# Value tiles in two alternating buffers, and a new order of jobs in the loop of a fused attention and mixture-of-experts kernel

## The reference

```python
xn = _layernorm(x, axis=-1)
x = x + _L0_attn_ref(xn, ...) + _L0_ffn_ref(xn, ...)

# _L0_attn_ref: 16 heads of 16, causal
score = softmax(Q @ K.T / sqrt(16) + mask);  out = (score @ V) @ WO

# _L0_ffn_ref: 16 heads of 64, 8 experts, top 2 of them
q, k = _rope(xn @ Wq), _rope(xn @ Wk)
gv = _gate(x, Wsel_v)                       # sigmoid, top-2 mask, (b, h, s, e)
v = jnp.einsum('bsd,bhse,hedp->bhsp', x, gv, Wv)
att = jax.nn.softmax(q @ k.T / np.sqrt(P), axis=-1)
o = jnp.einsum('bhst,bhtp->bhsp', att, v)
go = _gate(x, Wsel_o)
src2 = jnp.einsum('bhsp,bhse,hepd->bsd', o, go, Wo)
src = _ln(src + src2, ln1_g, ln1_b)
return _ln(src + relu(src @ W1 + b1) @ W2 + b2, ln2_g, ln2_b)
```

## Time and profile before

| | us |
|---|---|
| median of 3 runs (lowest, highest) | 3324.17 (3323.59, 3324.88) |
| the profiled execution, its own time | 3322.09 |
| span of its trace | 3320.0 |
| busy: PE, PE weight load | 3194.8 (96%), 2394.5 (72%) |
| busy: DVE, ACT, POOL | 2459.3 (74%), 2006.3 (60%), 1578.1 (48%) |

### The profile page before, as it was taken

One profiled execution on the slowest core, in us unless ns is written; L12 is line 12 of the kernel. 1 busy time (PEld: TensorE's weight loads), 2 busy tenths in 40 slices (PEclk: granted clock), 3 DMA queues, 4 the chain that ended last, 5 costly groups with the idle time before them and its releaser, 6 DMA issues.

```text
span 3320.0 us, 67575 instructions
## 1 busy us (share of the span) xinstructions
PE 3194.8 (96%) x19648; PEld 2394.5 (72%) x19648; DVE 2459.3 (74%) x4686; ACT 2006.3 (60%) x4635; POOL 1578.1 (48%) x1295
## 2 busy tenths in 40 slices
PE   4899999999999999999999999999999999998997
PEld 3677777777777777777777777777777777776887
DVE  7677777777777777777777777777777777776896
ACT  4566665666666666666666666666666666565443
POOL 5243554335543554435543454435544444435777
PEclk8999999999999999999999999999999999999999
DMA  5232332333233332333333332333323333333222
GB/s 191 72 89 70 104 94 75 85 92 99 70 86 77 100 98 67 89 88 99 81 75 85 93 99 70 86 95 95 86 67 89 88 99 82 74 83 107 85 84 77
DMA packets 116199, 294.21 MB, mean 89 GB/s; under 512 B 33856, under 2 KB 54592, under 8 KB 99776
## 3 DMA queue, kind: packets, MB, share of 16 engines
q1 hardware_dynamic: 116160, 293.73, 33.8%
...
## 4 chain that ended last, share of the span: by engine, by line
PE 71%; DVE 19%; issue 6%; ACT 1%; POOL 1%; DVEq 0%; DMA 0%; SPq 0%; POOLq 0%; ACTq 0%
PE bank L760 24%; PE bank L903 14%; PE bank L818 9%; PE bank L876 7%; PE bank L775 5%; DVE nmax L1350 4%; PE bank L847 2%; DVE vm L1371 2%; PE bank L780 2%; PE bank L888 2%; DVE vm L1414 2%; DVE uf L1458 2%; PE bank L1011 2%; PE bank L856 2%; DVE vm L1396 1%
## 5 line engine op out<-in xcount | busy, mean ns | idle before, releaser
L616 POOL TENSOR_TENSOR u_l<-uf,u_h 128x512 fp32r<-128x512 f32 x508 | 683.5, 1356 | 716.0 <-ACT u_h L1183 716.0
L1350 DVE TENSOR_REDUCE nmax<-bank 128x1 f32<-128x512 f32 (+3 forms) x1024 | 552.5, 580 | 374.2 <-PE bank L775 368.5
L760 PE MATMUL bank<-wv_h,xx 128*128 128x512 f32 x2048 | 745.6, 410 | 11.2 <-DVE vm L1371 5.9
L1093 ACT ACTIVATE probs<-bank,nmax 128x512 f32<-128x512 f32 (+3 forms) x1024 | 590.7, 610 | 258.5 <-DVE nmax L1350 258.5
L1183 ACT ACTIVATE u_h<-uf 128x512 fp32r<-128x512 f32 x508 | 320.5, 631 | 652.5 <-DVE uf L1458 504.5
L760 PEld LDWEIGHTS bank<-wv_h,xx 128*128 128x128 f32 x2048 | 386.7, 189 | 192.0 <-issue 69.3
L611 POOL TENSOR_TENSOR v_sb<-v_next,zero_hb 128x512 f32<-128x512 f32 x64 | 74.6, 1166 | 876.0 <-PE bank L876 876.0
L903 PE MATMUL bank<-u_h,wo_h 128*128 128x512 f32 x1016 | 429.8, 423 | 32.7 <-issue 27.2
L818 PE MATMUL bank<-ident_sb,probs 128*128 128x128 f32 x3328 | 451.1, 274 | 2.3 <-ACT pt_e L1113 1.2
L818 PEld LDWEIGHTS bank<-ident_sb,probs 128*128 128x128 f32 x3328 | 386.6, 141 | 69.1 <-issue 13.3
L1458 DVE TENSOR_TENSOR uf<-oo,go 128x512 f32<-128x512 f32 x508 | 420.3, 837 | 2.6 <-POOL u_l L616 0.4
...
## 6 DMA issues: line engine op xcount, KB each, us to landing
go<-go_d SPq DMA_DIRECT2D x256, 512.0 KB, 6.5
...
oo<-scale_d SPq DMA_DIRECT2D x128, 128.0 KB, 2.9
a_d<-a_out SPq DMA_DIRECT2D x128, 128.0 KB, 2.3
...
go_d<-go_turned SPq DMA_DIRECT2D x256, 8.0 KB
```

The lines of the kernel that those rows point to most:

```text
L616: nc.gpsimd.tensor_tensor(low, full, high.bitcast(f32), ALU.subtract).then_inc(ul_done, 1)
L760: last = nc.tensor.matmul(out, lhs, rhs, start=n == 1, stop=n == 3 * len(chunks))
L1093: nc.scalar.activation(probs[:, s % 2, j, 0:w], sbank[j][:, 0:w], ACT.Exp, bias=nmax[:, 2 * s + j:2 * s + j + 1], **kw).then_inc(exp_done, 1)
L1350: nc.vector.tensor_reduce(nmax[:, 2 * s + j:2 * s + j + 1], sbank[j][:, 0:w], AX.X, ALU.max, negate=True).then_inc(nmax_ready, 1)
```

## The change

Two things are changed.

**The value tiles.** `v_next` is gone and `v_sb` gets a leading index of two. VectorE adds up the values of the next pass straight into `v_sb[:, odd]`, and `AT` reads the other half. The copy `VC` on GpSimd and its semaphore are gone; `AT` waits for VectorE's sums themselves (`v_ready`). As the index is a constant in the code, the loops of TensorE and VectorE step by two and hold two bodies each, 31 times round instead of 62. ScalarE's, GpSimd's and SyncE's loops stay as they are.

**The tables.** The jobs are the same but for `VC`; their places are new. On TensorE by step:

| step | before | after |
|---|---|---|
| 0 | P0 P1 P2 P3 AT AC | P0 P1 P2 P3 AT |
| 1 | V0 V1 | AC V0 V1 J0 |
| 2 | J0 J1 | J1 |
| 3 | V2 J2 V3 | V2 J2 J3 |
| 4 | J3 J4 V4 | V3 |
| 5 | QK0 J5 QK1 | V4 QK0 J4 QK1 |
| 6 | V5 J6 V6 | J5 V5 V6 |
| 7 | V7 ST0 ST1 J7 | V7 ST0 J6 ST1 J7 |

VectorE has U2 in step 1 behind CH1 (before: step 2), V0 and U3 in step 2, U4 V1 U5 in step 3, V2 V3 in step 4, V4 U6 QL0 U7 QL1 in step 5, V5 V6 in step 6, V7 in step 7. ScalarE has PA between `a_out` (AC) and UH1 in step 0, nothing in steps 1 and 3, UH2 UH3 in step 2, UH4 UH5 in step 4, QH0 PB UH6 QH1 VA VN in step 5, UH7 in step 6. GpSimd has no part in the steps' softmax, so only its order counts: UL0 UL1 RP0 UL2 UL3 RP1 RS UL4 UL5 RA UL6 PC UL7 (before: VC UL0 UL1 UL2 RP0 UL3 RP1 UL4 RS RA UL5 UL6 PC UL7).

The diff, with the tables cut to a line or two:

```diff
--- before.py
+++ after.py
@@ -37,37 +37,37 @@
 BEHIND = ("AT", "AC", "ON", "U", "UH", "UL", "J", "YA")
 AHEAD = ("P", "V", "QK", "ST", "QH", "QL", "SO", "RP", "RS", "PA", "PB", "RA", "PC", "VN", "SQ", "SK", "EX", "CH")
 
-PE_FILL = [[("P", 0), ("P", 1), ("P", 2), ("P", 3), ("AT", 0), ("AC", 0)],
...
+PE_FILL = [[("P", 0), ("P", 1), ("P", 2), ("P", 3), ("AT", 0)],
+           [("AC", 0), ("V", 0), ("V", 1), ("J", 0)],
...
 V_ORDER = [(0, 0), (0, 1), (1, 0), (1, 1), (0, 2), (0, 3), (1, 2), (1, 3)]
 
@@ -185,8 +185,7 @@
         k_h = sb("k_h", [NP, S], f32r)
         k_l = sb("k_l", [NP, S], f32r)
         vm = sb("vm", [NP, 2, S])
-        v_next = sb("v_next", [NP, TT, 2, P])
-        v_sb = sb("v_sb", [NP, TT, 2, P])
+        v_sb = sb("v_sb", [NP, 2, TT, 2, P])
         va_next = sb("va_next", [NP, TT, 2, CA])
         va = sb("va", [NP, TT, 2, STRIP])
         nmax = sb("nmax", [NP, UNITS])
@@ -304,7 +303,6 @@
         stack_ready = sem("stack_ready")
         pool_step = sem("pool_step")
         v_ready = sem("v_ready")
-        vc_ready = sem("vc_ready")
         va_ready = sem("va_ready")
         part_high = sem("part_high")
         va_next_ready = sem("va_next_ready")
@@ -604,12 +602,7 @@
 
                 def do(job):
                     name, e = job
-                    if name == "VC":
-                        if kind != FIRST:
-                            pool.wait_ge(w_full, w_at(kind, it, ("AT", 0))[2] + 1)
-                        pool.wait_ge(v_ready, it * 8 + 8)
-                        nc.gpsimd.tensor_tensor(v_sb[:].rearrange("q t j c -> q (t j c)"), v_next[:].rearrange("q t j c -> q (t j c)"), zero_hb[:], ALU.add).then_inc(vc_ready, 1)
-                    elif name == "UL":
+                    if name == "UL":
                         of = it - 1 if kind != TAIL else it
                         pool.wait_ge(uh_done, of * E + e + 1)
                         full, high, low = u_tiles(kind, e)
@@ -793,7 +786,7 @@
                             mm = nc.tensor.transpose(o[:, (t % 2) * D + k * NP:(t % 2) * D + (k + 1) * NP], y_sb[:, b, k, t * NP:(t + 1) * NP], ident_sb[:])
                     mm.then_inc(c_full[f"y{i}"], 1)
 
-            def body(kind, it):
+            def body(kind, it, odd=0):
 
                 n = it + 1 if kind != PRO else 0
                 of = it if kind == TAIL else it - 1
@@ -868,12 +861,12 @@
                 def attend():
 
                     o = w_bank(("AT", 0))
-                    pe.wait_ge(vc_ready, of + 1)
+                    pe.wait_ge(v_ready, of * 8 + 8)
                     turned_before(6)
                     for k in range(TT):
                         for j in range(2):
                             for c in range(0, P, STRIP):
-                                mm = nc.tensor.matmul(o[j * P + c:j * P + c + STRIP, :], v_sb[:, k, j, c:c + STRIP], pt_e[:, j, k, :], start=k == 0, stop=k == TT - 1)
+                                mm = nc.tensor.matmul(o[j * P + c:j * P + c + STRIP, :], v_sb[:, odd if kind != TAIL else 1, k, j, c:c + STRIP], pt_e[:, j, k, :], start=k == 0, stop=k == TT - 1)
                     mm.then_inc(w_full, 1)
 
                 def attend_causal():
@@ -963,8 +956,9 @@
 
             body(PRO, 0)
             body(FIRST, 0)
-            with pe.Fori(1, PAIRS - 1) as it:
-                body(INNER, it)
+            with pe.Fori(1, PAIRS - 1, 2) as it:
+                body(INNER, it, 0)
+                body(INNER, it + 1, 1)
             body(LAST, PAIRS - 1)
             body(TAIL, PAIRS - 1)
 
@@ -1363,14 +1357,11 @@
 
                     j, t = V_ORDER[i]
                     o, free, count = w_filled(("V", i))
-                    if i == 0:
-                        if kind != PRO:
-                            dve.wait_ge(vc_ready, n)
                     g = gv[:, t, j:j + 1, :].to_broadcast([NP, P, E])
                     m = vm[:, i % 2].rearrange("q (c e) -> q c e", e=E)
                     nc.vector.tensor_tensor(m, o[:].rearrange("q (c e) -> q c e", e=E), g, ALU.mult).then_inc(free, 1)
                     dve.wait_ge(free, count)
-                    nc.vector.tensor_reduce(v_next[:, t, j, :], m, AX.X, ALU.add).then_inc(v_ready, 1)
+                    nc.vector.tensor_reduce(v_sb[:, odd, t, j, :], m, AX.X, ALU.add).then_inc(v_ready, 1)
 
                 def choose(half):
 
@@ -1486,9 +1477,10 @@
                         do(job)
 
             body(PRO, 0)
-            body(FIRST, 0)
-            with dve.Fori(1, PAIRS - 1) as it:
-                body(INNER, it)
+            body(FIRST, 0, 1)
+            with dve.Fori(1, PAIRS - 1, 2) as it:
+                body(INNER, it, 0)
+                body(INNER, it + 1, 1)
             body(LAST, PAIRS - 1)
             body(TAIL, PAIRS - 1)
 
```

More of the change, by code:

```diff
@@ L38 @@
 AHEAD = ("P", "V", "QK", "ST", "QH", "QL", "SO", "RP", "RS", "PA", "PB", "RA", "PC", "VN", "SQ", "SK", "EX", "CH")
-PE_FILL = [[("P", 0), ("P", 1), ("P", 2), ("P", 3), ("AT", 0), ("AC", 0)],
-           [("V", 0), ("V", 1)],
-           [("J", 0), ("J", 1)],
-           [("V", 2), ("J", 2), ("V", 3)],
-           [("J", 3), ("J", 4), ("V", 4)],
-           [("QK", 0), ("J", 5), ("QK", 1)],
-           [("V", 5), ("J", 6), ("V", 6)],
-           [("V", 7), ("ST", 0), ("ST", 1), ("J", 7)]]
-ACT_FILL = [[("P", 0), ("P", 1), ("P", 2), ("P", 3), ("EX", 0), ("UH", 0), ("AC", 0), ("UH", 1)],
-            [("VA", 0), ("PA", 0)],
-            [("UH", 2), ("UH", 3), ("VN", 0)],
+PE_FILL = [[("P", 0), ("P", 1), ("P", 2), ("P", 3), ("AT", 0)],
+           [("AC", 0), ("V", 0), ("V", 1), ("J", 0)],
+           [("J", 1)],
+           [("V", 2), ("J", 2), ("J", 3)],
+           [("V", 3)],
+           [("V", 4), ("QK", 0), ("J", 4), ("QK", 1)],
+           [("J", 5), ("V", 5), ("V", 6)],
+           [("V", 7), ("ST", 0), ("J", 6), ("ST", 1), ("J", 7)]]
@@ L51 @@
+ACT_FILL = [[("P", 0), ("P", 1), ("P", 2), ("P", 3), ("EX", 0), ("UH", 0), ("AC", 0), ("PA", 0), ("UH", 1)],
+            [],
+            [("UH", 2), ("UH", 3)],
+            [],
             [("UH", 4), ("UH", 5)],
-            [("UH", 6), ("PB", 0)],
-            [("QH", 0), ("QH", 1), ("UH", 7)],
-            [("SQ", 0), ("SK", 0)],
+            [("QH", 0), ("PB", 0), ("UH", 6), ("QH", 1), ("VA", 0), ("VN", 0)],
+            [("SQ", 0), ("SK", 0), ("UH", 7)],
             [("SO", 0), ("SO", 1)]]
@@ L56 @@
 DVE_FILL = [[("CH", 0), ("ON", 0), ("U", 0), ("U", 1)],
-            [("CH", 1)],
-            [("U", 2), ("V", 0), ("U", 3)],
-            [("V", 1), ("U", 4), ("V", 2), ("U", 5)],
-            [("V", 3), ("U", 6)],
-            [("V", 4), ("QL", 0), ("QL", 1), ("U", 7)],
-            [("V", 5), ("RECIP", 0)],
-            [("V", 6), ("V", 7), ("YA", 0)]]
-POOL_FILL = [[("VC", 0)],
-             [("UL", 0), ("UL", 1)],
-             [("UL", 2), ("RP", 0), ("UL", 3)],
-             [("RP", 1), ("UL", 4), ("RS", 0)],
-             [("RA", 0), ("UL", 5)],
-             [("UL", 6), ("PC", 0)],
-             [("UL", 7)],
+            [("CH", 1), ("U", 2)],
@@ new lines @@
+            [("U", 3), ("V", 0)],
+            [("U", 4), ("V", 1), ("U", 5)],
+            [("V", 2), ("V", 3)],
+            [("V", 4), ("U", 6), ("QL", 0), ("U", 7), ("QL", 1)],
+            [("RECIP", 0), ("V", 5), ("V", 6)],
+            [("V", 7), ("YA", 0)]]
+POOL_FILL = [[],
+             [],
+             [("UL", 0)],
+             [],
+             [("UL", 1), ("RP", 0), ("UL", 2), ("UL", 3), ("RP", 1), ("RS", 0), ("UL", 4), ("UL", 5), ("RA", 0), ("UL", 6), ("PC", 0), ("UL", 7)],
+             [],
+             [],
```

## The result

| | before | after |
|---|---|---|
| median (lowest to highest) | 3324.53 us (3323.59 to 3326.31) | 3245.57 us (3244.23 to 3245.74) |
| profiled execution, span | 3322.09, 3320.0 | 3245.74, 3243.9 |

The ratio is 0.976 (95% interval 0.9746 to 0.9777): 79 us less, where 51 were forecast. The time lies 1.6 us inside the lower end of the range (3244) and 2 us from the rival without a collision worth a wait (3248); how far that nearness is luck is worked out behind the experiments.

A forecast was written before the change was run, and what follows sets the result against it. TensorE was taken to set the pace, busy 45.88 of 46.50 us per pass. Terms -1.29 - 0.08 + 0.15 + 0.40 = -0.82 us, times 62 passes -51 us, gave 3273 us; range 3244 to 3316.

The forecast's parts named there:

- the rival without a collision worth a wait: Step 2: GpSimd and VectorE cause no wait ahead of scores(4); -1.22 us per pass, 3248 us; chance 0.20.
- three stalls: TensorE's waits at V3 (0.36 us), J4 (0.68) and QK1 (0.25) all go: -1.29 us per pass.
- loop's end: Transposes ending a pass: 0.15 us at the branch, paid only every second pass: -0.08 per pass, bounds 0 and 0.15.
- seams: TensorE: AC parted from AT, J6 between ST0 and ST1; slower first matmuls, +0.15 us per pass, bounds 0 and 0.25.
- P0 to P3, rest: Remaining work, including VectorE's dropped waits, SyncE's transfers and weights' splits: no change per pass, 0.
- wait ahead of scores(4): Step 2: exps(3) ends at 10.7, scores(4) wanted at 10.33; TensorE stands still +0.40 us per pass, bounds 0 and 1.7.
- narrow places: J2, J3, V1 and scores(3) in the new order: inputs about 0.5 to 0.6 us early, none late; a slip costs 0.1 to 0.5.
- Step 2, the collision: VectorE's CH1 operations stand still beside GpSimd's UL1 and RP0: 1.6 us more, at most 2.9, delaying exps(3).
- matter of 0.3 us: Step 2: whether VectorE and GpSimd meet in every pass or not hangs on about 0.3 us.
- By itself it is worth 0: GpSimd's copy VC, 1.17 us per pass: nothing on TensorE waits for it, so removing it alone gains 0.
- The longer loop: Rival: two-body loop on TensorE or VectorE no longer stays on chip, fetch at the branch; say 3350 us; chance 0.12.

The follow-up runs named there:

- j6_late: Kernel before with only J6 moved on TensorE from step 6 to step 7, between ST0 and ST1: 3308.1 us, ratio 0.995.
- buffers_only: Kernel after with the old tables, less VC (two value buffers, loops of two bodies), compared with before: 3294.7 us, ratio 0.991.
- copy_true: Kernel after plus an unread GpSimd addition at VC's old place, with operands of VC's kinds; compared with before: 3275.2 us, ratio 0.985.

## Why the prediction was right in direction and short in size

The pass of before from 1059.20 and the one of after from 1033.19, by distances of starts, in us:

| term | forecast | measured |
|---|---|---|
| three stalls | -1.29 | -1.22: V3's -0.26, J4's -0.69, around QK1 -0.27 |
| loop's end | -0.08 | -0.37 |
| seams | +0.15 | +0.23 |
| P0 to P3, rest | 0 | -0.02 |
| wait ahead of scores(4) | +0.40 | 0 in seven of eight, +1.13 in the eighth |
| pass | -0.82 | -1.38, mean of 61 passes -1.23 |

61 passes give -75.1 us, the last two -1.8, what stands ahead of the first AT -1.0, and behind the last +1.8: -76.1, the spans' difference. Of the 0.41 us by which the mean pass is shorter than forecast, the two terms of the sum that were mis-sized make 0.56, the wait ahead of scores(4) (0.40 instead of a mean of 0.13) and the loop's end (0.08 instead of 0.37); the seams and the stalls take 0.15 back. The rival without a collision worth a wait has the usual pass right in its mechanism; that its total (-1.22 per pass, measured -1.23) fits to the hundredth is luck, as the loop's end (-0.29) makes up for the eighth passes (+0.13), the seams (+0.08) and the stalls (+0.07).

- **The stalls**: right, each by its cause. J4's and QK1's came as written. V3's gave 0.26 and not 0.36: I counted its slow first matmul (0.51) as part of the wait, but V3 takes 1.48 in after too, now behind bf16 scores. None of the narrow places that I named slipped (J2 1.39, J3 1.41).
- **Step 2, the collision**: mis-sized, by 0.27 us in the mean, 17 us of the run. Place, engine and times were right (UL1 forecast from 4.8 to 6.1 after AT, measured 4.85 to 6.14), the size was not: 1.16 us instead of 1.6, because a RECIPROCAL with one input runs beside RP0's first half, and row_max(2) came 0.12 earlier. exps(3) was over at 10.10 and not 10.7, with scores(4) wanted at 10.33. A margin of 0.28 decided over 0.40 per pass; my "matter of 0.3 us" in the rival was right, the choice between them was not to be had from the rows. The eighth passes I did not see. I wrote that the weights' splits stand behind UL7 and that UL7 runs at the same time as before; it starts 33.3 us behind AT instead of 32.4, in a pass that is 1.4 us shorter. So the last split ends 2.1 us behind the next AT (401.38 against 399.27), where it ended 0.1 ahead of it before, and meets CH0.
- **The loop's end**: mis-sized, 0.37 instead of 0.08, 18 us of the run. I read the 0.15 as the price of a branch and halved it. The branch costs nothing when the sequencer comes to it early enough; what had held it up was SO1, and J6 between ST0 and ST1 took that away in all passes. j6_late, the passes of buffers_only without a branch and the equal lengths of after's passes with and without one show it.
- **"By itself it is worth 0"**: a wrong step, though the sum doesn't rest on it. I asked who waits for the copy, and nobody does. I should have asked what runs beside it. The sum was spared because its terms held what the copy does: the whole of V3's stall was counted as gone, and step 2 was laid out with the pair U0, U1 already short. The copy stretches that pair by 0.33 us, which was V3's wait in the old order (20 of the 31 us of buffers_only). In the new order row_max(2) follows U1 at once, so the pair's end decides which operations of CH1 meet UL1 and RP0; copy_true shows what that is worth, 30 us. Whoever had kept the copy because it is worth 0 would have got 3276 and not 3246.
- **The longer loop**: no fetch per pass. 21 packets in each queue shown. By the rule of the Trainium skill (Runtime: NRT & Kernel Launch, "Instruction fetch mechanics"), with room for 2048 and 512 instructions, both loops fit, and the trace agrees with that (some 1280 and 270 instructions of TensorE and VectorE per turn, register operations included).
